# Four seams of a four-layer kernel: what ends the first block, where a bias is added, in which order loads leave, and where a table product stands

## The reference, cut to what matters

```python
xn = layernorm(x); s = attention_like(xn); g = silu(ffn(xn)); x = x + s * g
```

## Time and profile before

| what | us |
|---|---|
| median of 3 runs | 1045.13 (1040.69 to 1045.65) |
| the profiled execution | 1047.63, of which its span 1045.9 |
| TensorE busy in the span | 980.6 |
| VectorE busy | 690.5 |
| ScalarE busy | 487.9 |
| GpSimd busy | 279.2 |

### The profile page before, as it was taken

One profiled execution on the slowest core, in us unless ns is written; L12 is line 12 of the kernel. 1 busy time (PEld: TensorE's weight loads), 2 busy tenths in 40 slices (PEclk: granted clock), 3 DMA queues, 4 the chain that ended last, 5 costly groups with the idle time before them and its releaser, 6 DMA issues. The chain is left out here.

```text
span 1045.9 us, 13773 instructions
## 1 busy us (share of the span) xinstructions
PE 980.6 (94%) x4708; PEld 599.6 (57%) x4708; DVE 690.5 (66%) x1080; ACT 487.9 (47%) x1036; POOL 279.2 (27%) x244
## 2 busy tenths in 40 slices
PE   5999989989999999998999999988999999999997
PEld 2555554365665666644645555655667676555554
DVE  2789867279999999768345545665666614567653
ACT  3632233799887886321145455535666611111112
POOL 0000000008887888310022332103545510000000
PEclk9999999999999999999999999989999999999999
DMA  4123114040000000055044443220000001211101
GB/s 128 42 65 95 51 55 131 1 123 21 21 21 21 28 14 1 1 159 171 11 132 113 101 97 75 51 61 1 1 1 2 1 1 31 60 31 30 30 1 40
DMA packets 53952, 52.84 MB, mean 51 GB/s; under 512 B 9864, under 2 KB 48873, under 8 KB 53889
## 3 DMA queue, kind: packets, MB, share of 16 engines
q1 hardware_dynamic: 48352, 46.00, 14.9%
q0 software_dynamic: 3072, 4.20, 2.6%
q10 hardware_dynamic: 2464, 1.84, 0.6%
HBM read 44.45 MB, written 5.47 MB: 48 GB/s over the span
## 5 line engine op out<-in xcount | busy, mean ns | idle before, releaser
L1085 POOL TENSOR_TENSOR seen<-state,c_row 128x512 f32<-128x512 f32 x128 | 160.5, 1276 | 103.2 <-DVE state L1105 75.9
L1105 DVE TENSOR_TENSOR_SCAN state<-decay,banks 128x512 f32<-128x512 f32 x128 | 155.3, 1216 | 14.8 <-issue 7.3
L2470 PE MATMUL banks<-xnT,weight 128*128 128x512 f32 x256 | 115.0, 592 | 1.0 <-PEq L2197 1.0
L1043 ACT ACTIVATE weighed_x<-dx_tok,b_tok 128x512 f32<-128x512 f32 x124 | 87.7, 709 | 25.7 <-PE banks L1215 24.4
L2204 POOL TENSOR_TENSOR prob<-prob,inverse 128x512 f32<-128x512 f32 x64 | 65.2, 1039 | 113.4 <-DVE inverse L2289 113.4
L1053 ACT ACTIVATE decay<-delta_pairs,A 128x510 f32<-128x510 f32 x128 | 90.5, 707 | 6.2 <-DVE state L1105 6.2
L1215 PEld LDWEIGHTS banks<-ident,weighed_x 128*128 128x128 f32 x512 | 58.6, 140 | 59.2 <-ACT weighed_x L1043 33.3
L2511 DVE TENSOR_TENSOR inter<-gelu,banks 128x512 f32<-128x512 f32 x32 | 22.0, 687 | 96.7 <-ACT gelu L2502 96.1
L2502 ACT ACTIVATE gelu<-banks 128x512 f32<-128x512 f32 x32 | 19.1, 597 | 138.2 <-PE banks L2470 138.2
L1215 PE MATMUL banks<-ident,weighed_x 128*128 128x128 f32 x512 | 80.1, 279 | 2.3 <-DVE state L1105 2.3
L2470 PEld LDWEIGHTS banks<-xnT,weight 128*128 128x128 f32 x256 | 48.6, 190 | 49.3 <-issue 47.8
(11 more groups left out here) (382 smaller groups left out, 1781.6 us busy)
## 6 DMA issues: line engine op xcount, KB each, us to landing
prob_row<-probs_dram SPq DMA_DIRECT2D x8, 512.0 KB, 3.8
c_row<-c_dram SPq DMA_DIRECT2D x32, 128.0 KB, 3.0
slot_wide_w<-in_L_ffn_w_gate SPq DMA_DIRECT2D x16, 176.0 KB
slot_wide_w<-in_L_ffn_w_up SPq DMA_DIRECT2D x16, 176.0 KB
slot_down_w<-in_L_ffn_w_down SPq DMA_DIRECT2D x16, 176.0 KB
gate_up_w<-in_L_ffn_gate_up_w SPq DMA_DIRECT2D x8, 256.0 KB, 2.9
delta_pairs<-conv_in SPq DMA_DIRECT2D x8, 256.0 KB
w_WqT<-in_L_attn_W_q SPq DMA_DIRECT2D x1, 2048.0 KB, 10.6
```

Of the source, the lines that this page charges most:

```text
L1043: nc.scalar.activation(weighed[:, v % 2, tile, :, j, :], dx_tok[:, 4 * p + tile, :].rearrange("p (g e) -> p g e", g=groups), ACT.Identity, ...
L1085: nc.gpsimd.tensor_tensor(seen[:, u % ring, :], state[:, u % ring, :], c_row[:, v % 4, :], ALU.mult).then_inc(seen_ready, 1)
L1105: nc.vector.tensor_tensor_scan(state[:, u % ring, :], decay[:, u % ring, :, :].rearrange("p b t -> p (b t)"), banks[:, 4 + u % 2, :], 0.0, ...
L2470: last = nc.tensor.matmul(banks[:, 4 + 2 * half + j, :], weight[:, s, j, k, tile * P:(tile + 1) * P], xnT[:, k, cols[half]], start=(k == 0 ...
```

## The change

- The first block: `earlier` counts with the small weights of layer 0, so the block waits for the identity alone, and `norm_stage` of layer 0 waits for `earlier`.
- Layer 0: the router's product for two tiles follows each of the four groups of `W_in`. `s_tok` with the bias is gone: a new `add_bias` adds gate times bias to x, on VectorE for pairs 0 and 1 and on GpSimd for pairs 2 and 3, and `add_gated` reads the product from PSUM.
- Layer 1: the loads are split into four lists, in the order `norm_w`; `W_in`, `W_skip`; five small ones; `W_d1`, `W_d2`, `W_BC`, `gate_w`, `expert_weight`. Each list has its own semaphore, waited for where it is used.
- Layer 2's routing: `before` is 6; both `keep_busy` are gone; the table products stand ahead of the shared expert's down product; SP doesn't wait for this layer's weights before it loads the next one's, and doesn't wait for the store of the shared output, for which the first scatter waits instead.

```diff
@@ norm_stage, SP @@
-                    for dst, src in late[0]:
-                        sp.dma_start(dst, src).then_inc(late[1], DMA)
+                    for part, sem in zip(late[::2], late[1::2]):
+                        for dst, src in part:
+                            sp.dma_start(dst, src).then_inc(sem, DMA)
...
+def add_bias(nc, waits, engine, b, x_tok, scratch, gated, bias, gate_ready, done):
+    pair = slice(2 * b, 2 * b + 2)
+    waits.wait_ge(gate_ready, b + 1)
+    engine.tensor_tensor(scratch[:, pair, :], gated[:, pair, :], bias[:, :].unsqueeze(1).broadcast_to([P, 2, D]), ALU.mult
+                         ).then_inc(done, 1)
+    waits.wait_ge(done, 2 * (b % 2) + 1)
+    engine.tensor_tensor(x_tok[:, pair, :], x_tok[:, pair, :], scratch[:, pair, :], ALU.add).then_inc(done, 1)
...
@@ recurrent_layer_stage, TensorE @@
-                for t in range(NT):
-                    for k in range(KD):
-                        last = nc.tensor.matmul(banks[:, 7, t * experts:(t + 1) * experts], ...
+                        for t in range(4 * part + 2 * half, 4 * part + 2 * half + 2):
+                            for k in range(KD):
+                                last = nc.tensor.matmul(banks[:, 7, t * experts:(t + 1) * experts], ...
@@ GpSimd @@
+                for b in range(2, NT // 2):
+                    add_bias(nc, pool, nc.gpsimd, b, x_tok, s_tok, gated, w["b_out"], gate_ready, bias_by_pool)
@@ VectorE @@
+                for b in range(2):
+                    add_bias(nc, dve, nc.vector, b, x_tok, s_tok, gated, w["b_out"], gate_ready, bias_by_vector)
                 for b in range(NT // 2):
                     dve.wait_ge(mixed, 2 * b + 2)
-                    nc.vector.tensor_tensor(s_tok[:, 2 * b:2 * b + 2, :], banks[:, 4 + b, :]..., w["b_out"]..., ALU.add)...
-                    dve.wait_ge(s_ready, b + 1)
-                    add_gated(nc, dve, b, x_tok, s_tok[:, 2 * b:2 * b + 2, :], gated, gate_ready, x_ready, stats)
+                    if b < 2:
+                        dve.wait_ge(bias_by_vector, 2 * b + 2)
+                    else:
+                        dve.wait_ge(bias_by_pool, 2 * b - 2)
+                    add_gated(nc, dve, b, x_tok, banks[:, 4 + b, :]..., gated, gate_ready, x_ready, stats)
...
@@ scan_prepare_stage @@
-                pe.wait_ge(*late_weights)
+                pe.wait_ge(*first_weights)
                 (products by W_in and W_skip)
+                pe.wait_ge(*rest_weights)
...
+                act.wait_ge(*small_weights)          # before A_log
+                dve.wait_ge(*small_weights)          # first instruction of VectorE
...
@@ route_stage @@
-    before = 3
+    before = 6
...
-                sp.wait_ge(*rest_weights)
                 for dst, src in next_loads:
                     sp.dma_start(dst, src).then_inc(next_loaded, DMA)
+                sp.wait_ge(stored, 2 * DMA)
                 sp.wait_ge(y_ready, NT // 2)
-                sp.dma_start(by_token(y_dram[0:N, :]), y_shared[:, :, :]).then_inc(stored, DMA)
-                sp.wait_ge(stored, 3 * DMA)
+                sp.dma_start(by_token(y_dram[0:N, :]), y_shared[:, :, :]).then_inc(y_stored, DMA)
...
-                keep_busy(nc, banks[:, 1, :], ident, 5)
...
+                (wait for the constants and the masks, table products, table_done)
                 pe.wait_ge(dve_ended, ended(len(jobs) - 1, True))
                 (down product of the shared expert)
-                (wait for the constants and the masks, table products, table_done)
-                keep_busy(nc, banks[:, 1, :], ident, 3)
...
@@ attention_and_expert_stage, scatter @@
+                    else:
+                        pool.wait_ge(y_stored, DMA)
...
@@ build, first block @@
+        loads0.append(earlier_load)
...
-                sp.dma_start(earlier...).then_inc(consts_loaded, DMA)
-                sp.wait_ge(consts_loaded, 2 * DMA)
+                sp.wait_ge(consts_loaded, DMA)
```

More of the change, by code:

```diff
@@ L699, with scan_prepare_stage @@
 MI = INNER // P
-def scan_prepare_stage(nc, w, late_weights, later, later_loaded, xnT, x1T, ident, banks, keep, rows, y):
+def scan_prepare_stage(nc, w, weights, later, later_loaded, xnT, x1T, ident, banks, keep, rows, y):
     taps, experts = 4, 8
+    first_weights, small_weights, rest_weights = weights
     skip, xs, delta_pairs, A, diag, fold, b_tok, dx_tok = keep
@@ L1465, in _ @@
                     job(n)
+                pe.wait_ge(consts_ready, 5)
+                pe.wait_ge(slots_ready, 1)
+                for e in range(EXPERTS2):
+                    for t in range(NT):
+                        last = nc.tensor.matmul(banks[:, 0, e * INFO:(e + 1) * INFO], one_hot[:, t, e, :],
+                                                info[:, t, e, :], start=(t == 0), stop=(t == NT - 1))
+                last.then_inc(table_done, 1)
                 pe.wait_ge(dve_ended, ended(len(jobs) - 1, True))
@@ L2679, in load_layer1, with add @@
 def load_layer1(m, first, A, up_w):
-    w, loads, late, later = {}, [], [], []
-    def add(name, shape, src, to=loads, m=m):
+    w, loads, late, small, rest, later = {}, [], [], [], [], []
+    def add(name, shape, src, to, m=first):
         w[name] = m.sbuf("w1_" + name, shape)
         to.append((w[name][:], src))
-    add("W_out", [P, MI, D], by_feature(A["L1_attn_W_out"]), later)
-    add("down_w", [P, INTER1 // P, D], by_feature(A["L1_ffn_down_w"]), later)
-    add("ln_gamma", [P, D], A["L1_ffn_ln_gamma"].partition_broadcast(P), later)
@@ L2690, in load_layer1 @@
-    add("ln_beta", [P, D], A["L1_ffn_ln_beta"].partition_broadcast(P), later)
+    add("W_out", [P, MI, D], by_feature(A["L1_attn_W_out"]), later, m)
+    add("down_w", [P, INTER1 // P, D], by_feature(A["L1_ffn_down_w"]), later, m)
+    add("ln_gamma", [P, D], A["L1_ffn_ln_gamma"].partition_broadcast(P), later, m)
+    add("ln_beta", [P, D], A["L1_ffn_ln_beta"].partition_broadcast(P), later, m)
     w["up_w"] = up_w
     later.append((up_w, by_feature(A["L1_ffn_up_w"])))
-    add("A_log", [P, MI * STATES], A["L1_attn_A_log"], m=first)
@@ L2694, in load_layer1 @@
-    add("W_D", [P, MI], A["L1_attn_W_D"], m=first)
-    add("norm_w", [P, KD], A["L1_attn_norm_w"], m=first)
-    add("W_in", [P, KD, INNER], by_feature(A["L1_attn_W_in"]), late, first)
-    add("W_skip", [P, KD, INNER], by_feature(A["L1_attn_W_skip"]), late, first)
-    add("conv_w", [P, MI, 4], A["L1_attn_conv_w"].rearrange("(k p) a j -> p k (a j)", p=P), m=first)
-    add("conv_b", [P, MI], A["L1_attn_conv_b"], m=first)
-    add("W_d1", [P, MI, P], by_feature(A["L1_attn_W_d1"]), late, first)
@@ L2701, in load_layer1 @@
-    add("W_BC", [P, MI, 2 * STATES], by_feature(A["L1_attn_W_BC"]), late, first)
-    add("W_d2", [P, 1, INNER], by_feature(A["L1_attn_W_d2"]), late, first)
-    add("b_d2", [P, MI], A["L1_attn_b_d2"], m=first)
-    add("gate_w", [P, KD, 8], by_feature(A["L1_ffn_gate_w"]), late, first)
-    add("expert_weight", [P, KD, D], by_feature(A["L1_ffn_expert_weight"]), late, first)
-    return w, loads, late, later
+    add("norm_w", [P, KD], A["L1_attn_norm_w"], loads)
+    add("W_in", [P, KD, INNER], by_feature(A["L1_attn_W_in"]), late)
@@ new lines, in load_layer1 @@
+    add("W_skip", [P, KD, INNER], by_feature(A["L1_attn_W_skip"]), late)
+    add("conv_w", [P, MI, 4], A["L1_attn_conv_w"].rearrange("(k p) a j -> p k (a j)", p=P), small)
+    add("conv_b", [P, MI], A["L1_attn_conv_b"], small)
+    add("W_D", [P, MI], A["L1_attn_W_D"], small)
+    add("A_log", [P, MI * STATES], A["L1_attn_A_log"], small)
+    add("b_d2", [P, MI], A["L1_attn_b_d2"], small)
+    add("W_d1", [P, MI, P], by_feature(A["L1_attn_W_d1"]), rest)
+    add("W_d2", [P, 1, INNER], by_feature(A["L1_attn_W_d2"]), rest)
@@ L2709, in load_layer2 @@
+    add("W_BC", [P, MI, 2 * STATES], by_feature(A["L1_attn_W_BC"]), rest)
+    add("gate_w", [P, KD, 8], by_feature(A["L1_ffn_gate_w"]), rest)
+    add("expert_weight", [P, KD, D], by_feature(A["L1_ffn_expert_weight"]), rest)
+    return w, loads, late, small, rest, later
 def load_layer2(m, A):
```

45 lines of the change are left out of this document (20 added, 25 removed).

## The result

The changed kernel takes 1038.95 us (median of 16 runs, 1036.11 to 1042.79), the kernel before 1044.43 beside it (16 runs, 1040.69 to 1047.56): 0.9945 of the time, 95% interval 0.993 to 0.996. It is faster, by 5.5 us and not by the 12 to 13 that were forecast, and 1038.95 lies 0.45 above the range. The profiled execution of after took 1039.74 (span 1037.9, mean granted clock 0.984), that of before 1047.63 (1045.9, 0.989): 7.9 apart. So the profiled pair shows 2.4 more than the medians do: before's profiled execution stood 3.2 above its own median, after's 0.8.

What follows compares the result with a forecast made beforehand. TensorE, busy 94% of the span, was taken as the bound, with losses at seams. Terms 3.9 + 0.8 + 0.3 + 2.95 + 6.0 - 0.3 = 13.65 us gave 1034.0 from the profile, 1031.5 from the median; forecast 1032.5, range 1028 to 1036.

Steps and rivals of the forecast that it cites:

- First block, 3.9: First block: without the wait for `earlier` the next block starts at 8.2 instead of 12.23; 3.9 us gained.
- Router, 0.8: Layer 0: router matmuls between the groups of `W_in` avoid the slow clock in `W_ga`; 0.8 us gained.
- a fall elsewhere in the chunks: Layer 0's router chunks: the clock falling at another place among them, the step's lower bound of -0.5 us.
- Bias, 0.3: End of layer 0: bias added ahead shortens VectorE's work, but TensorE's identity matmuls limit the gain to 0.3 us.
- rival 2: Seam after layer 0 is VectorE's, so its whole 2.8 us comes; 1030 us, chance 0.05.
- Loads, 2.95: Layer 1: loads in order of use start TensorE 1.2 us earlier and remove a clock fall; 2.95 us gained.
- Routing, 6.0: Layer 2's routing: real work replaces identity matmuls and idling, one clock fall of 1.7 expected; 6.0 us gained.
- Store over the seam, 0.3: Seam after routing: the 1 MB store runs beside the first expert weights and first gather; 0.3 us lost.
- rival 4: Layer 2's attention: without identity matmuls TensorE stays at 1.2 GHz; eight stretches cost about 27 us, twelve give 1053; chance 0.03.
- rival 3: Start of the experts: store, weights and gather stand in one line, 3.9 us more lost; 1036.5 us, chance 0.08.
- Rival 1: Clock fall in layer 1 stays (1.75 less), routing has three slow stretches (3.4 less); about 1037.6 us, chance 0.17.

Runs made afterwards that it cites:

- after_again: The changed kernel profiled once more with nothing edited; that execution took 1039.19 us.
- rest_only: The changed kernel with the routing stage as in the kernel before; 1037.62 us, 0.9923 of the kernel before.
- fill_masks: The changed kernel plus 6 identity matmuls in TensorE's idle ahead of the wait for the masks; 1037.73 us.
- tables_behind: The changed kernel with the table products back behind the shared expert's down product, no identity matmuls added; 1034.47 us.
- tail_busy: The changed kernel plus one identity matmul behind the down product, in the idle before the attention stage; 1039.70 us.
- early_down: The changed kernel with one identity matmul and three of eight down-product tiles moved ahead of the table products; 1033.54 us.
- woven: The changed kernel with one identity matmul and four down-product tiles before the masks' wait, then one down matmul after each two experts' tables; 1031.49 us.
- all_filled: woven plus one identity matmul behind the down product and two ahead of expert 0 in layer 0; 1028.94 us.
- before_again: The kernel before profiled once more with nothing edited; that execution took 1042.6 us.
- route_only: The kernel before with only the routing's four edits; 1046.91 us, 1.0014 of the kernel before.

## Why the prediction was wrong, step by step

Measured in the profiled executions, which are 7.9 apart where 13.65 was forecast.

- **First block, 3.9.** Right in cause: left at 8.00 (8.2 forecast; 7.88 to 9.08 in the nine profiles with the new block). The transposes behind it took 3.12 instead of 2.05, about 1 where 0.1 was allowed, so 3.3 had come when `W_in` started and 3.4 at the router's logits. With the router 4.2 of 4.7 came.
- **Router, 0.8.** It came (3.40 ahead at the logits, 4.21 at `turns`), and `W_ga` in 3.70 says that chunks of 0.94 us of narrow matmuls are followed by no fall. It was given back twelve microseconds later: TensorE reaches expert 0 with 2.26 us idle instead of 1.67, and the clock falls there, 1.7 lost. The bound "a fall elsewhere in the chunks" named the mechanism and the wrong place. The fall is in after, after_again, rest_only, fill_masks, tables_behind and tail_busy, not in early_down and woven, whose code in layer 0 is the same; all_filled shortens the idle to 0.54, and it isn't there either, which after those two proves little.
- **Bias, 0.3.** 0.25. TensorE's tail was the limit, as argued, and rival 2 falls. But VectorE was done only 0.6 us before it, where 2.5 was forecast, for GpSimd slowed it: adds of 1.05 and 1.61 instead of 0.69, both with two operands in SBUF and beside a GpSimd instruction, while the multiply by a PSUM operand kept its 0.67 beside another. Each slowed add ends about 0.55 after the GpSimd instruction it met. The Trainium skill, SBUF — State Buffer, section SBUF: two separate sides, says that a VectorE instruction with two SBUF inputs and a GpSimd instruction that reads SBUF exclude each other for their whole length. These rows agree.
- **Loads, 2.95.** 2.93 in the profile, in part by luck. `W_in` starting 1.2 earlier is structure. The missing fall, 1.73, was credited against one execution: in before_again it is missing too, and the convolution starts 4.37 after `W_in`, as in after (4.34). With the old loads it stands in two profiles of three (before, route_only), with the new ones in one of nine (all_filled, 6.03), so the shorter gap may help, but it is not worth the full 1.73. The prediction had priced this part as 1.2 or 2.95 "by luck", but put the full 2.95 into the sum. The Trainium skill, TensorE: Matmul & The Clock Gate, Part 1, says that the monitor behind the clock runs freely. These profiles agree with that: the fall comes in one execution and not in the next. The gap rule that the prediction drew from the earlier trace rows, no fall behind 1.4 to 1.7 us of idling, doesn't hold: 1.61 ahead of the scores was followed by one in six profiles.
- **Routing, 6.0: the step that failed.** Masks at 499.60 where 499.66 was forecast (505.3 less the 5.64 gained by then), the idle 5.90 where 5.9 was. Then "I expect one fall" met 10.2 us at 1.2 GHz: 2.9 on the down product instead of 1.7, 0.2 on the tables. 4.76 came in this profile. And of those 4.76, 3.0 had been before's own falls at 476 and 524, which stood in "4.93 less 3.6" and in the 528.16 against which the end was measured. They come in some executions only: before_again doesn't have them (67.14 from the router to the scores, not 70.14; 65.38 after), rest_only does (70.12). Without them what is left is 1.8. The order of tables and down product was worked out rightly, but never compared with the other one, which needs 4.3 us less up to the first gathered tile (69.99 in tables_behind against 74.30).
- **Store over the seam, 0.3: the other half of it.** 2.7 lost, by the clock and not by the store. "Three identity matmuls stand at that stage's start", the argument against rival 4, was true and useless: they ran at 1.2 GHz, 4.23 us for 2.74. The removed `keep_busy` had carried the clock over the seam (idle 0.42 there, 1.61 now). Rival 4 had mechanism and place right and the length wrong: 6.8 us at the lower clock, which cost 3, not 27. With the clock kept the gather is what comes next: TensorE waits 1.70 for it in tail_busy, where it lands after 6.8 us instead of 5.5, but 0.28 in all_filled. So rival 3 may have a part, well under its 3.9; no run takes the store away.

Rival 1 (the clock takes its part, 1037.6, chance 0.17) is the nearest. Its three stretches behind the idle came; its fall in layer 1 didn't in either profile of after, and the loss in the attention stage was rival 4's. So its time is near partly by luck, and it too left in the sum the falls that before has in some executions only. 1.8 from the routing stage less about 3.1 behind it (8.92 from scores to gathered tile against 5.78) is -1.3; route_only measured -1.5.

Not settled: why the layer-0 fall of 44 is absent from early_down and woven, whether the stretches of 680 and 696 are anyone's fault, and whether the tables' few columns are the cause of the fall behind them or only its company: woven changes the spacing of the tables and where the down product stands in one edit, and has two profiles (with all_filled) to show for it.

## What to carry to other kernels

Before crediting the removal of a slow-clock stretch, profile the kernel twice or compare mean clocks over its runs: here the time without clock loss went from 1034.2 to 1022.8 (good to some 3 us), and the loss to the lower clock rose from 11.0 to 16.4. Rows of matmuls of a few columns count as busy in a profile; where all 128 table matmuls ran on end, the lower clock followed in 9 of 10 profiled executions, and where they were spread between full-width matmuls in neither of two. And before changing the order of two products, ask which engine is the long chain at that point: work that could be done while that engine is still busy should not be queued behind it.

## What had not been expected of the hardware

- Filling an idle with full-width identity matmuls right up to 128 matmuls of 6 columns didn't keep the clock behind them (fill_masks: 13.60 for the down product, as without), nor did 4.2 us of real work (early_down: 30 down matmuls in 9.75).
- An idle of 1.6 us followed by score matmuls on 32 partitions was followed by 6.8 us at 1.2 GHz in six profiles of six; with an idle of 0.75 there was no fall in two of two.
- The same kernel's two profiled executions can lie 5.0 us apart though almost nothing differs but where the clock falls: 1.5 lost and 1.6 won in layers 0 and 1 put the router of layer 2 at 458.44 and 458.46, and 3.4 of the difference lie in the 75 us behind it.
